# Causal attention scores on 32 rows of a head, two heads at a time, in place of masked copies of q

## The reference, cut to what matters

```python
q = (h @ wq.T).reshape(Bx, Tx, NH, HD).transpose(0, 2, 1, 3)     # NH = 4, HD = 16
k = (h @ wk.T).reshape(Bx, Tx, NKV, HD).transpose(0, 2, 1, 3)    # NKV = 2
q = q * cos + _rotate_half(q) * sin
k = k * cos + _rotate_half(k) * sin
scores = jnp.einsum('bhtd,bhsd->bhts', q, k) / jnp.sqrt(jnp.float32(HD))
scores = jnp.where(causal[None, None], scores, jnp.float32(-1e+30))
att = jax.nn.softmax(scores, axis=-1)
y = jnp.einsum('bhts,bhsd->bhtd', att, v)
x = x + y @ wo.T
```

## Time and profile before

| | us |
|---|---|
| median of 3 runs | 5979.6 (5971.81 to 5990.2) |
| the profiled execution | 5986.29 |
| its span, first to last instruction | 5984.5 |
| first unit's row maximum to the last one's, `causal` | 4776.1 to 5387.4 |
| scores, L1055, PE busy in that stage | 302.6 |

### The profile page before, as it was taken

One profiled execution on the slowest core, in us unless ns is written; L12 is line 12 of the kernel. 1 busy time (PEld: TensorE's weight loads), 2 busy tenths in 40 slices (PEclk: granted clock), 3 DMA queues, 4 the chain that ended last, 5 costly groups with the idle time before them and its releaser, 6 DMA issues. The chain is left out here.

```text
span 5984.5 us, 99589 instructions
## 1 busy us (share of the span) xinstructions
PE 4887.7 (82%) x28585; PEld 2788.7 (47%) x28585; DVE 4128.0 (69%) x7553; ACT 3987.4 (67%) x5466; POOL 3739.8 (62%) x3407
## 2 busy tenths in 40 slices
PE   2688888888888888888788888888888599997999
PEld 1344444444444444444444444444444365555777
DVE  2577777777777777777777777777777466665443
ACT  1577777787777777777777777777777444442222
POOL 4577777777777777777777777777777344440111
PEclk9899999999999999999999999999999699998999
DMA  0000000000000000000000000000000000000000
GB/s 7 21 8 7 9 9 7 7 7 7 7 7 9 9 7 7 7 7 7 7 9 9 7 7 7 7 7 7 9 9 6 9 1 2 2 1 16 5 5 6
DMA packets 34205, 45.60 MB, mean 8 GB/s; under 512 B 24521, under 2 KB 24585, under 8 KB 34058
## 3 DMA queue, kind: packets, MB, share of 16 engines
q1 hardware_dynamic: 32010, 43.49, 2.7%
q0 software_dynamic: 2048, 0.14, 0.1%
HBM read 39.40 MB, written 4.19 MB: 7 GB/s over the span
## 5 line engine op out<-in xcount | busy, mean ns | idle before, releaser
L588 PE MATMUL banks<-ident,att 128*128 128x128 f32 x8192 | 1141.4, 286 | 422.6 <-DVE ag L520 253.2
L588 PEld LDWEIGHTS banks<-ident,att 128*128 128x128 f32 x8192 | 937.3, 146 | 1016.4 <-DVE ag L520 615.7
L630 PE MATMUL banks<-kT,qT 128*128 128x512 f32 x2048 | 1136.9, 654 | 282.3 <-DVE mx L549 273.2
L390 POOL TENSOR_TENSOR sinb<-sinb,ag 128x1024 f32<-128x1024 f32 x512 | 1287.8, 2519 | 79.3 <-ACT sinb L461 65.0
L540 DVE SCALAR_TENSOR_TENSOR mag<-near,mag 128x512 f32<-128x512 int32 x1024 | 846.2, 831 | 484.6 <-POOL near L406 475.1
L400 POOL TENSOR_SCALAR mag<-mag 128x512 f32<-128x512 f32 x1024 | 691.8, 680 | 575.7 <-DVE mag L540 541.0
L647 PE MATMUL outp<-sinb,vo 128*64 128x512 f32 x2048 | 1045.4, 635 | 0.0
L647 PE MATMUL outp<-work,vo 128*64 128x512 f32 x2048 | 1045.4, 635 | 0.0
L406 POOL TENSOR_SCALAR near<-mag 128x512 int32<-128x512 f32 x1024 | 796.3, 778 | 356.8 <-ACT mag L479 294.2
L479 ACT ACTIVATE mag<-banks 128x512 f32<-128x512 f32 x1024 | 599.0, 592 | 276.7 <-PE banks L630 275.7
L497 DVE TENSOR_TENSOR work<-banks,work 128x1024 f32<-128x1024 f32 x512 | 625.4, 1222 | 189.1 <-ACT work L455 186.4
(11 more groups left out here) (197 smaller groups left out, 6520.3 us busy)
## 6 DMA issues: line engine op xcount, KB each, us to landing
x<-xT_dram SPq DMA_DIRECT2D x128, 256.0 KB, 3.6
xT_dram<-xT SPq DMA_DIRECT2D x8, 256.0 KB, 2.9
out<-hres SPq DMA_DIRECT2D x8, 256.0 KB, 3.0
base<-in_L_tok_turns,idx POOLq DMA_INDIRECT x64
wqk<-in_L_attn_Wq SPq DMA_DIRECT2D x64, 16.0 KB
wqk<-in_L_attn_Wk SPq DMA_DIRECT2D x64, 16.0 KB
wqk<-in_L_attn_bq SPq DMA_DIRECT2D x64, 0.2 KB
wqk<-in_L_attn_bk SPq DMA_DIRECT2D x64, 0.2 KB
```

Source lines behind the costliest of these rows:

```text
L390: nc.gpsimd.tensor_tensor(sinb[:, k % RING], sinb[:, k % RING], ag[:, k], ALU.mult).then_inc(tmul, 1)
L588: mm = nc.tensor.matmul(turn_pair(k)[:, c, i * P:(i + 1) * P], att[:, p, 4 * half + i, kt * P:(kt + 1) * P], ident[:], is_transpose=True, ...
L630: nc.tensor.matmul(score_bank(n), qT[:, p, (n // 2) * P:(n // 2 + 1) * P], kT[:, p, (n % 2) * 512:(n % 2 + 1) * 512], start=True, stop=Tru ...
```

## The change

q is kept twice, for the batch that is computed and the next, as k was (`q_r` is now [P, 2, S]). The four masked copies, the mask and the semaphore `spread` are gone. The score matmul takes rows 32h to 32h+31 of q and k. At every even step PE waits for both PSUM slots and then issues the scores of units n and n+1, which are two heads of one query block and so lie in two different groups of 32 rows; at odd steps it issues none. Where a unit is wider than 512 keys, the two units' first 512 come first, then the two rests. POOL's sum for q moves from step 17 to 18, that for k from step 27 to 22.

```diff
-        q_r = sb("c_q", [P, S])
-        q_h = sb("c_qh", [P, 2, NH, S])
+        q_r = sb("c_q", [P, 2, S])
...
-        ROPE = {17: "q", 19: 0, 21: 1, 23: 2, 25: 3, 27: "k"}
+        ROPE = {18: "q", 22: "k"}
...
-                    nc.gpsimd.tensor_tensor(q_r[:], q_r[:], q_s[:], ALU.add).then_inc(summed, 1)
-                elif part == "k":
+                    nc.gpsimd.tensor_tensor(q_r[:, par], q_r[:, par], q_s[:], ALU.add).then_inc(summed, 1)
+                else:
...
-                else:
-                    held(pool, summed, b + 1)
-                    nc.gpsimd.tensor_scalar(q_h[:, par, part], q_r[:], own[:, part:part + 1], 1.0,
-                                            ALU.mult, ALU.mult).then_inc(spread, 1)
...
-                    if exists(b):
+                    if exists(b) and n % 2 == 0:
                         if n == 0:
-                            wait(pe, spread, NH * (b + 1))
+                            wait(pe, summed, b + 1)
                             wait(pe, roped, b + 1)
-                        freed(*last[score_slot(n)])
+                        for m in (n, n + 1):
+                            freed(*last[score_slot(m)])
+                            last[score_slot(m)] = (b, m)
                         pe.nop(nofuse=True)
-                        qt, h = UNITS[n]
-                        s = sc[:, score_slot(n)]
+                        qt = UNITS[n][0]
                         for c in range(0, (qt + 1) * P, 512):
                             e = min(c + 512, (qt + 1) * P)
-                            mm = nc.tensor.matmul(s[:, c:e], q_h[:, par, h, qt * P:(qt + 1) * P], k_r[:, par, c:e],
-                                                  start=True, stop=True, skip_group_check=True)
-                        mm.then_inc(sc_done, 1)
-                        last[score_slot(n)] = (b, n)
+                            for m in (n, n + 1):
+                                rows = slice(32 * UNITS[m][1], 32 * UNITS[m][1] + 32)
+                                mm = nc.tensor.matmul(sc[:, score_slot(m), c:e], q_r[rows, par, qt * P:(qt + 1) * P],
+                                                      k_r[rows, par, c:e], start=True, stop=True,
+                                                      skip_group_check=True)
+                                if e == (qt + 1) * P:
+                                    mm.then_inc(sc_done, 1)
```

More of the change, by code:

```diff
@@ L704, in causal @@
         xsT = sb("c_xsT", [D, S])
-        q_r = sb("c_q", [P, S])
-        q_h = sb("c_qh", [P, 2, NH, S])
+        q_r = sb("c_q", [P, 2, S])
         k_r = sb("c_k", [P, 2, S])
-        own = sb("c_own", [P, NH])
         q_s = sb("c_qs", [P, S])
@@ L725, in causal @@
         names = ("w_in zeroed consts wmul ln sqd rooted scaled xT xT_sb proj cosd sind roped pt_done pt_sb pt_sb2 "
-                 "sc_done vd v_sb maxed expd yd yT_sb wd w_sb summed spread recip normed wo_add").split()
+                 "sc_done vd v_sb maxed expd yd yT_sb wd w_sb summed recip normed wo_add").split()
         (w_in, zeroed, consts, wmul, ln, sqd, rooted, scaled, xT, xT_sb, proj, cosd, sind, roped, pt_done, pt_sb, pt_sb2,
-         sc_done, vd, v_sb, maxed, expd, yd, yT_sb, wd, w_sb, summed, spread, recip, normed,
+         sc_done, vd, v_sb, maxed, expd, yd, yT_sb, wd, w_sb, summed, recip, normed,
          wo_add) = (ctx.enter_context(nc.semaphore("c_" + n)) for n in names)
@@ L811, in _ @@
                                     base=0, pattern=[[-1, P]], channel_multiplier=1).then_inc(consts, 1)
[L813 to L819, removed]
+            pool.wait_ge(consts, 3)
             def rope(b, par, part):
@@ L874, in values_out @@
                                      ACT.Copy).then_inc(v_sb, 1)
-            act.wait_ge(consts, 6)
+            act.wait_ge(consts, 3)
             tokens_out(0)
@@ L949, in table @@
             def table(b, par, i):
-                dst, tab, done = ((q_r[:], cs, cosd), (q_s[:], sn, sind), (k_r[:, par], cs, cosd),
+                dst, tab, done = ((q_r[:, par], cs, cosd), (q_s[:], sn, sind), (k_r[:, par], cs, cosd),
                                   (k_s[:], sn, sind))[i]
@@ L959, in _ @@
                 table(0, 0, i)
-            dve.wait_ge(consts, 6)
+            dve.wait_ge(consts, 3)
             def body(b, par):
@@ L999, in _ @@
             pe.wait_ge(wmul, 3)
-            pe.wait_ge(consts, 6)
+            pe.wait_ge(consts, 3)
             def freed(b, item):
```

## The result

The changed kernel takes 6189.0 us (median of 4 runs) against 5975.7 us (4 runs of the kernel before), a ratio of 1.035 (95% interval 1.0328 to 1.0371). The forecast was 6014, the range ended at 6085. The direction was right and the size was six times too small.

A forecast was written before the change was run, and what follows sets the result against it. PE was taken as nearly full in the causal stage, with DVE's drain rounds close behind. Blocks +30 us over seven batches, last batch -1, clock +5: +34 on the median 5979.6 gives 6014 us, range 5972 to 6085.

The forecast's parts named there:

- PE's freed time does not become time of the kernel: Causal stage: waits added by pairing outweigh PE's saved score time; blocks sum to +4.3 us a batch.
- the row groups overlap: Score matmuls: a pair's two 32-row groups run side by side, taking 15.4 us a batch off PE.
- the wait for the cosine and sine products: Blocks 3 and 4: pairs are issued only after DVE's product on pieces p0 to p3; +2.3 and +0.9 us.
- G - E: Pairs without a piece: drain-to-next-drain wait less DVE's own rest of the round; 0.1 us narrow to 0.8 wide.
- block 7 gains: Widest block: relief from late scores outweighs the wait; 11.6 against 12.88 us, -1.3.
- The first rival: PE's queue decides, so blocks 3 to 5 and 7 shrink, 7.7 us a batch; 5926 us, chance 0.13.
- G: End of one drain to start of the next when scores are issued only after it; 0.78 to 2.28 us by width.
- the second rival: Row groups do not run side by side; 0.85 us in eight wide pairs a batch; 6078 us, chance 0.15.
- the chain through the values: Block 5, first pair: v product, transposes, values, ACT's copies, then the wait for scores; 7.3 us.
- 1.67 ns a column: PE time per score column, with a filling of about 0.17 us a matmul; scores 30.7 us a batch.
- the term "Clock": Causal stage: less dense PE gets a lower clock at times, 0.7 us in each of seven batches; +5 us.
- The third rival: Gaps between pairs keep PE's clock near 0.78 for good, 11 us a batch; 6100 us, chance 0.07.

The follow-up runs named there:

- pair64_fill1: Kernel before with pairs in two groups of 64 rows, masked copies kept, plus one useless 128-row matmul a unit; 6064 us, 1.0069.
- pair64: Kernel before with units issued in pairs in two groups of 64 rows, masked copies kept; 6091 us, 1.017.
- pair128: Kernel before with the pairing alone, masked copies and 128 rows kept, so a pair's units run one after the other; 6101 us, 1.019.
- fill3: Kernel after plus three useless 128-row bf16 matmuls of 512 columns ahead of each unit's transposes; 6079 us, 1.011.
- rows32_single: Kernel after with its pairing undone: one unit at a time, old waits, scores still on 32 rows; 6363 us, 1.063.
- rows64_single: Kernel before, one unit at a time, score matmuls cut to 64 rows, masked copies kept; 6174 us, 1.031.
- fill3_rows32: Kernel after plus three useless matmuls a unit, these on 32 rows instead of 128; 6380 us, 1.060.

## Why the prediction was wrong

The table sets the forecast of each block against pairs with the clock nearly held (pair64_fill1, batch from 5234.51; block 7 there 11.97) and against the kernel after (batch from 5294.19). "Before" is the earlier trace rows; times are in us. Blocks 0 and 2 differ between batches of the kernel before by 2 us, so single rows of theirs say less than the others.

| block | before | forecast | pairs, clock held | after | clock after |
|---|---|---|---|---|---|
| 2 | 7.98 | 9.2 | 9.68 | 11.87 | 0.61 |
| 3 | 9.24 | 11.5 | 11.24 | 17.20 | 0.50 |
| 4 | 11.56 | 12.5 | 12.33 | 19.38 | 0.50 |
| 5 | 11.52 | 12.5 | 13.75 | 16.07 | 0.61 |
| 6 | 10.96 | 11.45 | 11.67 | 13.83 | 0.75 |
| 7 | 12.88 | 11.6 | 11.97 | 12.26 | 0.78 |

**Right: PE's freed time does not become time of the kernel.** With the row groups side by side and the clock up, the pairs are still slower than before: 0.7% in pair64_fill1, added matmuls included, near the 0.6% that the forecast gives. The steps hold one by one: the row groups overlap; the wait for the cosine and sine products costs blocks 3 and 4 what was said, within 0.3 us; the plain pairs pay G - E (0.91 measured, 0.92 in the sum); block 7 gains. Blocks 4 and 7 of pair64 show the same without added work. The first rival (PE's queue decides, 5926) is out.

**Too low: block 2, and not block 5.** pair128 has both blocks with the clock at 1.00:

```profile
5255.52:5265.21 9.69, 5.88 (x34) 3.45 (x33) 5.09 (x16) 4.49 (x11) 3.69 (x6) 1.00 0.01 2
5291.52:5305.57 14.05, 11.33 (x86) 7.80 (x85) 7.05 (x19) 5.58 (x12) 5.38 (x7) 1.00 0.00 1
```

Block 2 has no unit wider than 512, and is 0.5 over the 9.2 forecast, as in the table: unit 10 drains after 5.69 us (5.75 in the sum), but from the end of unit 11's drain to unit 12's it is 1.85 in pair64_fill1 where G had 1.43. Block 5 forecast at 12.5, with the second rival's 0.85 for each of its two pairs, is 14.2, and took 14.05: the estimate for the chain through the values was not too low (its terms add up to 7.4, not 7.3). The 13.75 in pair64_fill1 go with the clock of 0.88 there and the added matmuls; how much with each, no run parts. Blocks 0 and 1 together are 15.3 us there and 15.4 in the kernel after, against 14.6 before and 14.3 forecast, which is also not parted.

**Not exact: 1.67 ns a column.** With a filling of 0.17 it gives 1.02 us at width 512 but 0.81 at 384, where the row has 0.88. The difference is small against the rest.

**Wrong: the term "Clock", +5 us.** This is the step that failed: the term was mis-sized. The stage lost 216 us. The pairs with the clock nearly held lose 56 (666.3 against 610.0, one added matmul a unit included), so some 160 us go with the clock. Without any other change, fill3 brings back 134, although it adds work. I had looked for the clock's cause in idle time, as in the earlier trace rows, and priced one such stretch a batch. The rows that would have warned me were in sight: every score record before reads 128*128. The change altered that number, and I costed only the columns.

**The third rival had the right sign and the wrong mechanism.** It gave 0.07 to a clock that falls for good because of gaps, at 6100. pair128 has the gaps and keeps 0.97; rows32_single has none in blocks 3 and 4 and falls. Also its price was too low: it assumed 0.78 over the stage, which got 0.64, and the path has more PE in it once the clock is low, since PE then is nearly full again (97% busy in block 4).

**Pages against rows.** A pair in two row groups took 1.56 us where one after the other took 2.82. The Trainium skill, "TensorE: Matmul & The Clock Gate", part on packing small matmuls, states that matmuls in different row groups run together; the trace agrees. PE busy for 43 us stayed at 1.2 GHz. The Trainium skill, the same page, Part 1, describes the clock as following how busy PE has been; here it does not follow the busy time that the profile shows. The measurement decides.

**Open.** Zeros in q alone do not bring the clock down: the kernel before has 112 of its 128 rows zero in every score matmul and keeps 0.98. But k, the other operand, has values on 64 of those rows, 32 in rows64_single and 16 in rows32_single. For the score matmuls, rows addressed and rows with values in k are therefore not told apart; in fill3 and fill3_rows32 all rows hold ones. A change between 128-row and smaller matmuls does not decide it alone: the kernel after and fill3 have them at the same places (0.64, 0.98), and so have rows64_single and rows32_single (0.74, 0.61). How the clock weighs rows against time is not settled. Whether pairs on 32 rows with a held clock and no added work would also come out at about +0.7% is not known, since nothing else that holds the clock was found.

## What to carry to other kernels

Before cutting a matmul to fewer rows, look at the granted clock of its stretch and at what other work PE has there: on a PE that was nearly full, the fewer rows cost more in clock (some 160 us) than the columns saved. Issuing two units together also gives up double buffering, so compare, unit by unit, the time from the end of one drain to the next scores with what the draining engine still has to do. And read a busy share only beside the clock.

## What the runs showed of the hardware

- Score matmuls on 128, 64 and 32 rows, otherwise the same stage one unit at a time: granted clock 0.98, 0.74, 0.61; stage 610, 801, 984 us.
- Three added matmuls a unit to the kernel after: clock 0.98 on 128 rows, 0.63 on 32 rows; stage 692 and 987 us.
- PE was shown busy for 43 us on end and remained at 1.2 GHz (rows32_single, blocks 3 and 4).
- The float32 scores of two units in two groups of 64 rows take 1.56 us where one after the other takes 2.82 (width 768).
